# Starting the next tile's search earlier in a fused audio tower: similarities behind the search of the preceding tile, ranks behind the weights

## The chip, the cores and the metric

The kernel runs on one core of a Trainium2 chip. The metric is the device time of one execution in microseconds; less is better.

## The reference

The input is x, 16 batches of 750 x 64 float32. Per batch the model computes a token front end (four tanh layers, a convolution over 15 taps with stride 2, which leaves 375 tokens), a retention layer, a product-key attention layer, a layer with one step of test-time training, and a mixture of 8 experts. Each adds to the residual h. The change touches the third, and of it this part:

```python
sim = einsum('pbnhd,pkhd->pbnhk', q, pk_keys)          # 2 x 8 heads x 64 keys
scores, idx = top_k(sim, 16)                           # for each half
score = scores[0][..., :, None] + scores[1][..., None, :]
final_scores, pk_idx = top_k(score, 16)                # the best 16 of 256 pairs
final_scores = softmax(final_scores)
k = einsum('bnhk,bnhkd->bnhd', final_scores, keys_table[ind])
v = einsum('bnhk,bnhkd->bnhd', final_scores, values_table[ind])
attn = softmax(where(causal, einsum('bihd,bjhd->bhij', q, k), neg))
out = einsum('bhij,bjhd->bhid', attn, v) @ Wo
```

The table has 4096 rows of 64 for each of 8 heads. The training step's gradient is summed over all batches, so the last layers run only after the last batch, in a tail.

## The kernel before

**Dense instead of a gather.** Keys and values of the chosen rows are not gathered. For each head the 4096 weights of each of the 375 tokens are built densely, 128 table rows at a time (`CHUNKS` = 32), and multiplied with the table, which streams in by DMA in pieces of 8 chunks. Whether a row is chosen is told by its rank: for each first half of a key, how many second halves go with it. One chunk of one head is a *slot* (`dense_slot`), and a batch has 256 + 6 = 262 of them. A slot is on TensorE L491 (the second factor, spread out), L493 (minus a large number where the row isn't chosen), L505 (the table times the weighted rows of six slots earlier, two records) and L512 (the ranks, spread out for the next slot); on ScalarE L878 and L883; and on GpSimd L440, the product with the first factor. Slots need their head's four *factors* (`factor`: ranks, firsts and two of seconds), which TensorE transposes out of `ranks`, `firsts` and `seconds` between slots, as `factor_at` says. Each engine runs its own order, written by hand, and waits on semaphores.

**Choosing.** `pick_rows(b, t)` on VectorE works on one tile of 125 tokens; a batch has three. It is a generator, and each `yield` is a place at which other work may come between. Its steps are: the search in `rest`, the copy of the similarities (two rounds of max, index and replace over 16 groups, ending with pick step 3), the best 16 pairs (L1178 to L1202), their codes (L1205 to L1217), the ranks of four pairs of heads (L1225, three times L1231, L1235), and the weights (L1240 to L1261), which need ScalarE's exponentials (`soften`). The codes lie in one `codes` buffer and the ranks are worked out in one `picks` buffer. TensorE makes the similarities of a tile into the bank `sims` (L593), and ScalarE copies them into `rest` (`keep_similarities`, L922).

**The order of an iteration.** While batch b goes through its attention, batch b + 1 is prepared. One iteration on each engine is `attention(b)` and then `ahead(b + 2)`:
- `attention(b)`: eight heads of softmax attention over the keys and values that the slots made. In each head TensorE lays `STEPS_A` and `STEPS_B` slots beside its own work. The slots are those of batch b up to head 5, and of batch b + 1 from head 6 on (`NEXT_FROM`), which begins with `begin(b + 1)`: wait for the weights of its tile 2, and make the factors of its head 0. VectorE takes `PICKS_INSIDE` steps of tile 2 of batch b + 1 in each head.
- `prepare(b + 2)`: front end and retention, a chain of small steps through TensorE, ScalarE and VectorE. Between them come `FILL_PREPARE` slots of batch b + 1. On VectorE it begins with the squares L1112; the next instruction is the copy L1114 of the convolution's sums (L551), then the statistics, for whose deviation ScalarE waits in its order (L842).
- the similarities of tile 0, then `gradient(b)`, between whose steps come `FILL_GRADIENT` slots and seven steps of choosing of tile 0; its last sum is L1334.
- `FILL_FIRST` slots, the similarities of tile 1, `FILL_SECOND` slots, the similarities of tile 2. VectorE finishes tile 0 and then does all of tile 1.

The loop runs 14 times. `ahead(1)` stands before it, so there are 15 stages "ahead"; batch 0 is prepared and chosen first, with no slots to run beside it.

## Time and profile before

| | |
|---|---|
| median of 3 runs | 7954.98 us (7948.87 to 8025.97) |
| the profiled execution | 7943.69 us, span 7941.9 us |
| TensorE (PE) busy | 6697.2 us, 84% |
| ScalarE (ACT) busy | 5005.2 us, 63% |
| GpSimd (POOL) busy | 4498.3 us, 57% |
| VectorE (DVE) busy | 4120.9 us, 52% |
| mean granted TensorE clock | 0.941 |
| an iteration of the loop, from one L1292 to the next (3522.27 to 3994.78) | 472.5 us |

A busy share is a mean over stages with different limits. An iteration has an attention stage of about 200 us and an "ahead" of about 275 us, and each is read by itself.

### The profile page before, as it was taken

How to read it: one execution, taken by the hardware profiler on the slowest of the kernel's cores; microseconds unless marked ns; L12 is line 12 of the kernel's file. 1: busy time of each engine (PE TensorE's matmuls, PEld its weight loads, DVE VectorE, ACT ScalarE, POOL GpSimd, SP SyncE). 2: the span in 40 equal slices, each digit the busy share in tenths (PEclk: the TensorE clock that was granted, in tenths of full speed). 3: DMA queues.
4: the chain of work that ended last, by engine and by line, in shares of the span. 5: the costliest groups of instructions: out<-in, count | busy, mean ns of one | idle time of the engine just before them, and what ended most of it. 6: DMA issues, size and time to landing. Idle time of an engine off the chain costs nothing.

```text
span 7941.9 us, 139719 instructions
## 1 busy us (share of the span) xinstructions
PE 6697.2 (84%) x28800; PEld 3500.4 (44%) x28800; DVE 4120.9 (52%) x13711; ACT 5005.2 (63%) x10845; POOL 4498.3 (57%) x4108
## 2 busy tenths in 40 slices
PE   2789798897979889798888979889797988979977
PEld 1445354443535444353443535444353544435533
DVE  7472645627374472646537264562737447273146
ACT  0666576665757666576665657667575766667842
POOL 0575665656565565656556565565656556566610
PEclk9999899998999999899998989999898999999977
DMA  0111111111111111111111111111111111111100
GB/s 29 46 42 34 37 40 38 40 36 36 40 36 39 37 40 36 36 40 38 38 38 38 36 38 41 36 40 36 35 40 36 40 35 40 36 38 44 48 19 13
DMA packets 93887, 294.93 MB, mean 37 GB/s; under 512 B 17879, under 2 KB 26546, under 8 KB 92780
## 3 DMA queue, kind: packets, MB, share of 16 engines
q1 hardware_dynamic: 92748, 285.25, 11.2%
q8 instruction: 322, 5.28, 0.3%
q14 instruction: 529, 4.33, 0.2%
q10 hardware_dynamic: 288, 0.07, 0.0%
HBM read 280.68 MB, written 4.61 MB: 36 GB/s over the span
## 4 chain that ended last, share of the span: by engine, by line
PE 62%; DVE 27%; issue 6%; ACT 4%; DVEq 0%; ACTq 0%; POOL 0%; DMA 0%; SPq 0%; POOLq 0%
PE accu L505 24%; PE dense L491 7%; PE dense L512 7%; DVE picks L1231 6%; PE dense L493 6%; DVE picks L1225 4%; PE sims L623 2%; PE work L629 2%; PE sims L593 2%; DVE store L1235 2%; PE work L668 1%; DVE i L1173 1%; PE work L616 1%; PE work L551 1%; DVE picks L1205 1%
## 5 line engine op out<-in xcount | busy, mean ns | idle before, releaser
L440 POOL TENSOR_TENSOR dense_w<-dense_w,store 128x375 f32<-128x375 f32 x4096 | 4495.9, 1107 | 3092.4 <-ACT dense_w L878 3070.1
L505 PE MATMUL accu<-dense_w,store 128*128 128x375 f32 x8192 | 3365.4, 494 | 186.8 <-POOL dense_w L440 104.5
L883 ACT ACTIVATE past<-dense,edge 128x375 bf16<-128x375 f32 x4096 | 2351.8, 574 | 1195.5 <-PE dense L512 1172.5
L878 ACT ACTIVATE dense_w<-dense 128x375 f32<-128x375 f32 x4096 | 1955.5, 477 | 114.8 <-PE dense L493 107.0
L505 PEld LDWEIGHTS accu<-dense_w,store 128*128 128x128 f32 x8192 | 1430.1, 194 | 554.7 <-issue 334.9
L512 PE MATMUL dense<-store,hot 128*128 128x375 bf16 x4096 | 1338.0, 327 | 163.5 <-ACT past L883 159.4
L491 PE MATMUL dense<-store,spread 96*128 96x375 bf16 x4096 | 1353.1, 330 | 53.0 <-ACT dense_w L878 45.7
L493 PE MATMUL dense<-past,far 128*128 128x375 bf16 x4096 | 1356.8, 331 | 0.0
L512 PEld LDWEIGHTS dense<-store,hot 128*128 128x128 bf16 x4096 | 400.5, 98 | 1490.1 <-issue 1241.3
L491 PEld LDWEIGHTS dense<-store,spread 96*128 96x128 bf16 x4096 | 401.6, 98 | 839.4 <-issue 541.1
L1231 DVE TENSOR_TENSOR picks<-picks 125x2048 uint16<-125x2048 uint16 (+2 forms) x576 | 726.5, 1261 | 76.5
L593 PE MATMUL sims<-simw,n2T 64*125 64x512 f32 x192 | 151.1, 928 | 521.4 <-DVE store L1261 509.2
L1225 DVE TENSOR_TENSOR picks<-codes,keys 125x4096 uint16<-125x4096 uint16 x192 | 533.1, 2776 | 21.5
L493 PEld LDWEIGHTS dense<-past,far 128*128 128x128 bf16 x4096 | 405.3, 99 | 102.8 <-issue 29.9
L922 ACT COPY front<-sims 125x1024 f32<-125x1024 f32 x48 | 48.6, 1012 | 600.6 <-PE sims L593 600.6
L1271 DVE TENSOR_TENSOR shared<-sims,mask 125x750 f32<-125x750 f32 x64 | 59.9, 936 | 608.9 <-PE sims L623 608.9
L593 PEld LDWEIGHTS sims<-simw,n2T 64*125 64x125 f32 x192 | 47.2, 272 | 579.5 <-issue 577.6
L1292 DVE TENSOR_TENSOR h<-h_now,work 125x192 f32<-125x192 f32 x16 | 5.7, 354 | 564.9 <-PE work L677 564.9
L1235 DVE TENSOR_TENSOR store<-picks 125x256 bf16<-125x256 uint16 x192 | 190.4, 992 | 25.5
L629 PE MATMUL work<-shared 125*64 125x375 f32 (+2 forms) x768 | 190.7, 383 | 12.1 <-ACT shared L975 12.1
L623 PE MATMUL sims<-kvT,two_q 64*125 64x125 f32 (+2 forms) x768 | 194.6, 386 | 3.7 <-issue 2.5
L1281 DVE RECIPROCAL zs<-zs 125x3 f32<-125x3 f32 x128 | 22.4, 175 | 323.3 <-ACT prob_odd L944 177.0
(248 smaller groups left out, 6497.6 us busy)
## 6 DMA issues: line engine op xcount, KB each, us to landing
store<-in SPq DMA_DIRECT2D x513, 512.0 KB, 3.5
x_in<-in SPq DMA_DIRECT2D x16, 187.5 KB, 2.4
store<-in SPq DMA_DIRECT2D x1, 2048.0 KB, 8.7
queries_kept<-n3T SPq DMA_DIRECT2D x16, 93.8 KB, 3.7
h_saved<-h SPq DMA_DIRECT2D x16, 93.8 KB
store<-queries_kept SPq DMA_DIRECT2D x16, 93.8 KB, 2.3
store<-h_saved SPq DMA_DIRECT2D x16, 93.8 KB
out<-store SPq DMA_DIRECT2D x16, 93.8 KB
```

Of the source, the lines that this page charges most:

```text
L440: nc.gpsimd.tensor_tensor(dense_w[:, i % RING, :], dense_w[:, i % RING, :], first_of[:, i // CHUNKS, :], ALU.mult).then_inc(s["weighed"], 1)
L491: mm(to[:, 0:S], spread[0:3 * I1S, c % (CHUNKS // GROUPS), :], second_of[0:3 * I1S, c // (CHUNKS // GROUPS), h, :], start=True, stop=False)
L493: mm(to[:, 0:S], far[:], past[:, i % 2, :], start=False, stop=True).then_inc(s["spread"], 1)
L505: last = mm(accu[:, 0, 0:S], table[:, n % PIECE_RING, i % PIECE, :], dense_w[:, i % RING, :], start=(c == 0), stop=(c == CHUNKS - 1))
L512: mm(coded, hot[:, j % CHUNKS, :], ranksT[:, j // CHUNKS, :], start=True, stop=True).then_inc(s["coded"], 1)
L593: last = mm(sims[0:P, c, :], n2T[:, tile(t)], simw[:, c * 512:(c + 1) * 512], start=True, stop=True)
L623: last = mm(dst, qT[:, h % 2, tile(i)], kvT[0:D, h, 0:(i + 1) * P], start=True, stop=True)
L629: last = mm(work[D:128, 0, j * P:S], vo[:, j, h * D:(h + 1) * D], pT[:, min(j, 1), (0, 0, 2 * P)[j]:(S, 2 * P, S)[j]], start=(h == 0 and j ...
L878: fn(dense_w[:, i % RING, :], dense[:, n % 2, 0:S], ACT.Relu).then_inc(s["taken"], 1)
L883: fn(past[:, j % 2, :], coded, ACT.Relu, bias=edge[:, 0:1]).then_inc(s["past"], 1)
L1225: v.tensor_tensor(hit, codes[:, h:h + 2].unsqueeze(3).broadcast_to([P, 2, 2, SUB, K]), keys[:].unsqueeze(1).unsqueeze(1).broadcast_to([P, ...
L1231: v.tensor_tensor(hit[:, :, :, :, 0:m], hit[:, :, :, :, 0:m], hit[:, :, :, :, m:2 * m], ALU.min).then_inc(s["pick_step"], 1)
```

## The change

- `similarities(b, t)` for t = 1 and 2 waits for pick step 3 of tile t - 1 (its search is over) instead of its weights, the end of all its steps.
- `pick_rows`: the ranks of heads 0 and 1 stay where they were, then come the weights, and then the ranks of heads 2 to 7. A pair of heads' ranks is now an xor, one minimum and one TENSOR_REDUCE (minimum over 8), where it was an xor and four minima. `PICK_STEPS` goes from 33 to 25.
- Tile 2: 17 of its 23 steps lie inside attention, 2 or 3 a head. The other six, the ranks of heads 2 to 7, follow the squares in the next `prepare` on VectorE.
- `factor_at`: the factors of head 1 stay at slots 0 to 6; those of heads 2 to 7 begin at slot 30 (`LATER_FROM`) instead of 8. For heads 2, 4 and 6 TensorE waits for the ranks of tile 2.
- The slots are laid out anew: 29 in a preparation (36 before), 30 in a gradient (37), 48 + 64 around the similarities (26 + 43), 10 in each of heads 0 to 5 (12), 19 of the next batch in attention (36).
- The similarities of tile 1 stand 4 slots behind the gradient, those of tile 2 another 62 slots on, and 46 slots follow them. `soften` of tile 0 comes 8 slots behind the first, of tile 1 14 slots behind the second.

```diff
--- before.py
+++ after.py
@@ -35,33 +35,33 @@
 SPREAD_LAG, SUM_LAG, RING = 2, 6, 6
 SLOTS = STEPS + SUM_LAG
 FACTORS = 4
-PREPARED_EVERY = 2
+PREPARED_EVERY, LATER_FROM = 2, 30
 PIECE = 8
 PIECES = STEPS // PIECE
 PIECE_RING = 4
 I1S = 32
 GROUPS = SUB // I1S
 TAG = 256
-PIECES_A, PIECES_B = 9, 14
-PICK_STEPS = 13 + 5 * (H // 2)
+PIECES_SOON = 17
+PICK_STEPS = 13 + 3 * (H // 2)
 FAR = 1024.0
-FILL_PREPARE = (4, 3, 3, 4, 5, 4, 4, 4, 5)
-FILL_GRADIENT = (3, 6, 5, 6, 6, 6, 5)
+FILL_PREPARE = (2, 2, 2, 3, 4, 4, 4, 4, 4)
+FILL_GRADIENT = (2, 4, 4, 5, 5, 5, 5)
 PICKS_GRADIENT = (1, 1, 1, 1, 1, 1, 1)
-FILL_FIRST = (8, 18)
-FILL_SECOND = (24, 19)
+FILL_FIRST = (4, 8, 36)
+FILL_SECOND = (18, 14, 32)
 FILL_VO, FILL_QUERY, FIRST_HEAD = (2, 2, 2), 2, 4
-STEPS_A = (6, 6, 6, 6, 6, 6, 8, 8)
-STEPS_B = (6, 6, 6, 6, 6, 6, 6, 6)
+STEPS_A = (5, 5, 5, 5, 5, 5, 5, 4)
+STEPS_B = (5, 5, 5, 5, 5, 5, 4, 3)
 NEXT_FROM = 6
-FILL_LAST = (3, 5)
-PICKS_INSIDE = (4, 4, 4, 4, 4, 3, 0, 0)
+FILL_LAST = (1, 2)
+PICKS_INSIDE = (3, 3, 3, 3, 3, 2, 0, 0)
 OWN = sum(FILL_VO) + FILL_QUERY + FIRST_HEAD + sum(STEPS_A[:NEXT_FROM]) + sum(STEPS_B[:NEXT_FROM])
 EARLY = sum(STEPS_A[NEXT_FROM:]) + sum(STEPS_B[NEXT_FROM:]) + sum(FILL_LAST)
 AHEAD = sum(FILL_PREPARE) + sum(FILL_GRADIENT) + sum(FILL_FIRST) + sum(FILL_SECOND)
 assert EARLY + AHEAD + OWN == SLOTS, (EARLY, AHEAD, OWN, SLOTS)
 assert EARLY + AHEAD - SUM_LAG >= (H - LATE) * CHUNKS
-assert sum(PICKS_GRADIENT) <= PIECES_A and sum(PICKS_INSIDE) == PIECES_A + PIECES_B
+assert sum(PICKS_INSIDE) == PIECES_SOON
 
 
 class Schedule:
@@ -82,6 +82,10 @@
 
     @staticmethod
     def factor_at(j):
+        if j >= LATER_FROM:
+            j -= LATER_FROM - FACTORS * PREPARED_EVERY
+        elif j >= FACTORS * PREPARED_EVERY:
+            return None
         n, odd = divmod(j, PREPARED_EVERY)
         n += FACTORS
         return divmod(n, FACTORS) if odd == 0 and n < H * FACTORS else None
@@ -469,6 +473,8 @@
                 return dense[:, n % 2]
 
             def factor(b, h, k):
+                if h >= 2 and h % 2 == 0 and k == 0:
+                    pe.wait_ge(s["pick_step"], (b * NT + (NT - 1)) * PICK_STEPS + 13 + 3 * (h // 2 + 1))
                 to = bank_free(b, ORDER.factor[h, k])
                 for t in range(NT):
                     if k == 0:
@@ -588,7 +594,7 @@
                     pe.wait_ge(s["nT_done"], b * 2 + 2)
                 else:
                     pe.wait_ge(s["sim_kept"], b * NT + t)
-                    pe.wait_ge(s["wgt_done"], b * NT + t)
+                    pe.wait_ge(s["pick_step"], (b * NT + (t - 1)) * PICK_STEPS + 3)
                 for c in range(2):
                     last = mm(sims[0:P, c, :], n2T[:, tile(t)], simw[:, c * 512:(c + 1) * 512], start=True, stop=True)
                 last.then_inc(s["sim_mm"], 1)
@@ -734,10 +740,11 @@
                     gradient(b - 2, True)
                 else:
                     fill(b - 1, sum(FILL_GRADIENT))
-                fill(b - 1, sum(FILL_FIRST))
+                fill(b - 1, FILL_FIRST[0])
                 similarities(b, 1)
-                fill(b - 1, sum(FILL_SECOND))
+                fill(b - 1, sum(FILL_FIRST[1:]) + FILL_SECOND[0])
                 similarities(b, 2)
+                fill(b - 1, sum(FILL_SECOND[1:]))
 
             def retrieve(p, chosen):
 
@@ -1020,13 +1027,14 @@
                 else:
                     fill(b - 1, sum(FILL_GRADIENT))
                 fill(b - 1, FILL_FIRST[0])
+                keep_similarities(b, 1)
+                fill(b - 1, FILL_FIRST[1])
                 soften(b, 0)
-                fill(b - 1, FILL_FIRST[1])
-                keep_similarities(b, 1)
-                fill(b - 1, FILL_SECOND[0])
+                fill(b - 1, FILL_FIRST[2] + FILL_SECOND[0])
+                keep_similarities(b, 2)
+                fill(b - 1, FILL_SECOND[1])
                 soften(b, 1)
-                fill(b - 1, FILL_SECOND[1])
-                keep_similarities(b, 2)
+                fill(b - 1, FILL_SECOND[2])
 
             def retrieve(p, chosen):
                 for l in range(2):
@@ -1107,9 +1115,11 @@
                                            ALU.subtract, ALU.mult)
                 last.then_inc(normalised, 1)
 
-            def prepare(b):
+            def prepare(b, picking=iter(())):
                 dve.wait_ge(s["tok_act"], b * 4 + 2)
                 v.scalar_tensor_tensor(tok[:, 1], tok[:, 1], core_s[:, 0:1], tok[:, 1], ALU.mult, ALU.mult).then_inc(s["tok_sq"], 1)
+                for _ in picking:
+                    pass
                 dve.wait_ge(s["conv"], b + 1)
                 v.tensor_copy(h0[:].rearrange("p t d -> p (t d)"), work[0:P, 0, 0:NT * D]).then_inc(s["h0_done"], 1)
                 dve.wait_ge(s["h0_done"], b + 1)
@@ -1220,22 +1230,22 @@
                     dve.wait_ge(s["taken"], (b - 1) * ORDER.items + ORDER.factor[H - 1, FACTORS - 1] + 1)
                 at_step(13)
                 yield
-                for h in range(0, H, 2):
-                    k = 14 + 5 * (h // 2)
+                def ranks_of(h):
+                    k = 14 + 3 * (h // 2)
                     v.tensor_tensor(hit, codes[:, h:h + 2].unsqueeze(3).broadcast_to([P, 2, 2, SUB, K]),
                                     keys[:].unsqueeze(1).unsqueeze(1).broadcast_to([P, 2, 2, SUB, K]),
                                     ALU.bitwise_xor).then_inc(s["pick_step"], 1)
                     at_step(k)
                     yield
-                    for m in (8, 4, 2):
-                        v.tensor_tensor(hit[:, :, :, :, 0:m], hit[:, :, :, :, 0:m], hit[:, :, :, :, m:2 * m],
-                                        ALU.min).then_inc(s["pick_step"], 1)
-                        k += 1
-                        at_step(k)
-                    v.tensor_tensor(ranks[:, t, h:h + 2, :].rearrange("p h (a i) -> p h a i", a=2), hit[:, :, :, :, 0], hit[:, :, :, :, 1],
+                    v.tensor_tensor(hit[:, :, :, :, 0:K // 2], hit[:, :, :, :, 0:K // 2], hit[:, :, :, :, K // 2:],
                                     ALU.min).then_inc(s["pick_step"], 1)
                     at_step(k + 1)
+                    v.tensor_reduce(ranks[:, t, h:h + 2, :].rearrange("p h (a i) -> p h a i", a=2), hit[:, :, :, :, 0:K // 2], AX_X,
+                                    ALU.min).then_inc(s["pick_step"], 1)
+                    at_step(k + 2)
                     yield
+
+                yield from ranks_of(0)
                 dve.wait_ge(s["fexp"], n)
                 v.tensor_reduce(esum[:, 0, :], wgt[:], AX_X, ALU.add).then_inc(s["fsum"], 1)
                 dve.wait_ge(s["fsum"], n)
@@ -1259,6 +1269,9 @@
                 v.tensor_copy(seconds[:, t, :, :, 1], halves_of).then_inc(s["part_step"], 1)
                 parts(4)
                 v.tensor_tensor(seconds[:, t, :, :, 2], halves_of, seconds[:, t, :, :, 1], ALU.subtract).then_inc(s["wgt_done"], 1)
+                yield
+                for h in range(2, H, 2):
+                    yield from ranks_of(h)
 
             def pick_some(picking, n):
                 for _ in range(n):
@@ -1334,8 +1347,8 @@
                 v.tensor_tensor(grads[:], grads[:], work[0:D + 1, 1, 0:2 * D], ALU.add).then_inc(s["g_done"], 1)
                 pieces()
 
-            def ahead(b, behind):
-                prepare(b)
+            def ahead(b, behind, picking=iter(())):
+                prepare(b, picking)
                 picking = pick_rows(b, 0)
                 if behind:
                     gradient(b - 2, True, picking)
@@ -1454,9 +1467,13 @@
                     pass
             ahead(1, False)
             with nc.vector.Fori(0, B - 2) as b:
-                attention(b, pick_rows(b + 1, 2))
-                ahead(b + 2, True)
-            attention(B - 2, pick_rows(B - 1, 2))
+                picking = pick_rows(b + 1, 2)
+                attention(b, picking)
+                ahead(b + 2, True, picking)
+            picking = pick_rows(B - 1, 2)
+            attention(B - 2, picking)
+            for _ in picking:
+                pass
             gradient(B - 2, False)
             attention(B - 1)
             gradient(B - 1, False)
```

## Rows read from the trace of the kernel before

**Rows 1.** The page: busy us of each engine (share of the span), instructions.

```profile
PE 6697.2 (84%) x28800; PEld 3500.4 (44%) x28800; DVE 4120.9 (52%) x13711; ACT 5005.2 (63%) x10845; POOL 4498.3 (57%) x4108
```

**Rows 2.** Waits, whole span: who waited for whom, us in total, times, longest.

```profile
PE sims L593 <- DVE store L1261: 509.2, 31, 55.9
...
DVE h L1114 <- PE work L551: 319.4, 16, 20.4
```

**Rows 3.** TensorE timeline, 3590 to 3800 us: start, duration, instruction, idle before.

```profile
3598.84 1.95 PE L593 MATMUL sims<-simw,n2T 64*125 64x512 f32 x4 [0.79 <-ACT n2T L918]
...
3716.02 3.74 PE L593 MATMUL sims<-simw,n2T 64*125 64x512 f32 x4 [15.23 <-DVE store L1261]
...
3792.64 3.74 PE L593 MATMUL sims<-simw,n2T 64*125 64x512 f32 x4 [12.38 <-DVE store L1261]
```

**Rows 4.** What ended TensorE's idle time before L593, from 420 us on.

```profile
  DVE store L1261: 397.5, 29
```

**Rows 5.** Windows of 10 us: busy time of each engine, PEclk, DMA.

```profile
3540.00:3550.00 10.00, 8.88 (x44) 4.51 (x43) 0.00 (x0) 8.64 (x17) 4.90 (x6) 1.00 0.17 52
...
3720.00:3730.00 10.00, 10.00 (x38) 5.03 (x36) 8.67 (x73) 7.22 (x15) 6.54 (x7) 0.84 0.00 1
...
3740.00:3750.00 10.00, 10.00 (x43) 4.73 (x42) 9.41 (x63) 7.93 (x18) 7.91 (x8) 1.00 0.17 54
...
3760.00:3770.00 10.00, 7.66 (x31) 3.47 (x29) 9.12 (x7) 6.11 (x13) 10.00 (x7) 1.00 0.17 55
...
3790.00:3800.00 10.00, 6.87 (x17) 4.03 (x18) 2.05 (x4) 1.44 (x2) 0.00 (x0) 0.50 0.02 7
3800.00:3810.00 10.00, 10.00 (x49) 5.82 (x48) 0.00 (x0) 6.35 (x13) 4.63 (x5) 0.91 0.15 52
```

**Rows 6.** VectorE timeline, 3655 to 3793 us.

```profile
3657.36 0.28 DVE L1334 TENSOR_TENSOR grads<-grads,work 65x128 f32<-65x128 f32 x1 [13.90 <-PE work L719]
...
3660.93 1.17 DVE L1178 TENSOR_TENSOR cand<-s 125x128 f32<-125x128 f32 x3
...
3711.58 0.29 DVE L1240 TENSOR_REDUCE esum<-wgt 125x8 f32<-125x128 f32 x1 [0.26 <-DVE store L1235]
...
3715.18 0.69 DVE L1261 TENSOR_TENSOR store<-ex,store 125x512 bf16<-125x512 f32 x1
3721.04 2.12 DVE L1152 MAX8 s<-front 125x8 f32<-125x64 f32 x16 [5.16 <-ACT front L922]
...
3736.76 1.79 DVE L1178 TENSOR_TENSOR cand<-s 125x128 f32<-125x128 f32 x8
...
3762.33 2.85 DVE L1225 TENSOR_TENSOR picks<-codes,keys 125x4096 uint16<-125x4096 uint16 x1
...
3771.03 2.86 DVE L1225 TENSOR_TENSOR picks<-codes,keys 125x4096 uint16<-125x4096 uint16 x1
...
3791.80 0.69 DVE L1261 TENSOR_TENSOR store<-ex,store 125x512 bf16<-125x512 f32 x1
```

**Rows 7.** VectorE timeline, 80 to 93 us, GpSimd idle.

```profile
86.75 2.29 DVE L1225 TENSOR_TENSOR picks<-codes,keys 125x4096 uint16<-125x4096 uint16 x1
89.07 1.22 DVE L1231 TENSOR_TENSOR picks<-picks 125x2048 uint16<-125x2048 uint16 x1
...
92.36 2.29 DVE L1225 TENSOR_TENSOR picks<-codes,keys 125x4096 uint16<-125x4096 uint16 x1
```

**Rows 8.** VectorE, groups by shape, whole span: count, busy us, mean ns.

```profile
L1209 DVE TENSOR_REDUCE over<-picks 125x128 f32<-125x2048 f32 x48 | 109.7, 2286 | 6.5 <-DVE picks L1205 4.3
```

**Rows 9.** GpSimd timeline, 3748 to 3792 us.

```profile
3748.09 4.51 POOL L440 TENSOR_TENSOR dense_w<-dense_w,store 128x375 f32<-128x375 f32 x3 [0.22 <-ACT dense_w L878]
3753.37 33.33 POOL L440 TENSOR_TENSOR dense_w<-dense_w,store 128x375 f32<-128x375 f32 x19 [0.76 <-ACT dense_w L878]
```

**Rows 10.** VectorE timeline, 3535 to 3563 us: a preparation.

```profile
3537.55 0.61 DVE L1112 SCALAR_TENSOR_TENSOR front<-front,core_s 128x375 f32<-128x375 f32 x1 [14.93 <-ACT front L898]
3558.40 0.36 DVE L1114 COPY h<-work 125x192 f32<-125x192 f32 x1 [20.23 <-PE work L551]
```

## Prediction, made before the run

> **What bounds the kernel now.** I read the page's engine line first: TensorE is busy for 84% of the span and no other engine for more than 63% [rows 1]. So the time is TensorE's work plus the 1245 us in which it stands, and the change can gain only from the latter, from slots that run slowly, or from a cold clock. Next I read the list of waits. One entry stands out for TensorE: the similarities (L593) wait 509.2 us in 31 pieces for L1261, the last step of the preceding tile's weights [rows 2]. The answer for L593 alone gives 397.5 us of these behind 420 us, in 29 pieces [rows 4]. So 111.7 us in two pieces belong to batch 0, where nothing else is there to run, and about 397.5 / 15 = 26.5 us to each of the 15 stages "ahead". In the one I follow, 15.23 and 12.38 us, 27.6 us together [rows 3].
>
> The TensorE and VectorE timelines of that stage show why. T0 is the end of the gradient's last sum, 3657.6 us. From there VectorE works without a break on tile 0 to 3715.9 (58.3 us) and, after 5.16 us in which the next similarities travel, on tile 1 from 3721.0 to 3792.5 (71.5 us) [rows 6]. TensorE has only 5 + 26 + 43 slots of dense work to lay beside this, and runs out twice. The windows show the second cost: after each stop PEclk is 0.50, then 0.84 and 0.91, against 1.00 elsewhere [rows 5], and the four matmuls of L593 take 3.74 us at 1.2 GHz, while those of tile 0, which had no long stop ahead of them, took 1.95 us [rows 3].
>
> A slot is five matmul records. In a quiet window 43 records pass in 10 us, so a slot takes 10 / 8.6 = 1.16 us. While VectorE makes ranks it is 31 records, 6.2 slots, with GpSimd busy for the whole window [rows 5]. GpSimd's timeline gives 19 products in 33.33 us, 1.75 us each, where the ranks are made, and two whole ones beside a 2.29 us TENSOR_REDUCE (three in 4.51 us, the first of which stood behind L1205) [rows 9]. So rank making slows the slots too.
>
> **The waits that move.** The similarities of tile 1 will wait for pick step 3 of tile 0, the end of the search. In the old trace tile 1's search ends 15.7 us after its start (3721.04 to 3736.76) [rows 6]; tile 0's ended 3.3 us behind T0 (the first L1178 starts at 3660.93), most of it having been done in the gradient's places. TensorE comes to the similarities of tile 1 at 5 + 4 = 9 slots, T0 + 11 us: no stop. For tile 2 see below.
>
> **Ranks.** A pair of heads takes 8.70 us beside the products (3762.33 to 3771.03) [rows 6] and 5.61 us with GpSimd idle (86.75 to 92.36) [rows 7]: its five two-input instructions lose 0.62 us each to sharing. Afterwards there is the xor, 2.29 us alone, the first minimum, 1.22 us alone [rows 7], and a TENSOR_REDUCE of 2048 elements to 256. That form isn't in the trace. The nearest is L1209, 2048 float32 elements to 128, 2286 ns over 48 instructions, most of them beside products [rows 8]. Its bounds: 1.2 us, if 16-bit input halves it as it does the minima, and 4.6 us, twice L1209, if runs of 8 out of 16 are slow; I take 2.3. A pair then takes about 5.9 us alone and 2.29 + 1.22 + 2.3 + 2 x 0.62 + gaps = 7.2 us beside products.
>
> The row on L1209 shows a reduction of the same length in 2.29 us whether GpSimd works or not. The Trainium skill, "VectorE: DVE Perf Modes", the rule table for kernel authors, calls tensor_reduce the slowest VectorE operation and advises against it on a hot path. By that rule this edit should lose. The three instructions that it replaces take 5.61 - 2.29 - 1.22 = 2.1 us alone and 2.1 + 3 x 0.62 = 4.0 us beside products [rows 6, 7], so against 2.3 us the rule holds in batch 0 and fails everywhere else. The Trainium skill, "GPSIMD Engine Reference", says that GpSimd's memory interface is shared with VectorE's two-input instructions; GpSimd's 1.75 us against two whole products in one reduction agrees.
>
> **The stage ahead, afterwards.** VectorE from T0: tile 0 takes 58.3 - 4 x 8.7 + 4 x 7.2 = 52.3 us, and tile 1 starts at once, for its similarities are long there. Tile 1's search ends at T0 + 52 + 16 = 68. TensorE reaches the similarities of tile 2 after 5 + 4 + 8 + 36 + 18 = 71 slots: at least 71 x 1.16 + 2 = 84 us, and with rank making at 1.7 us a slot about T0 + 97. No stop, with 16 to 29 us to spare. Tile 1's other work is 71.5 - 34.8 = 36.7 us. Its weights now need ScalarE's exponentials, which come 14 slots later, at about T0 + 115, so VectorE stands some 20 us there; then 4.3 us of weights (3711.58 to 3715.9) and three pairs, 21.6 us, end at T0 + 142. TensorE needs the 117 slots, T0 + 162, before the softmax asks for VectorE. The wait costs nothing; its margin is 20 us. This stage took 139 us (T0 to the end of L593 at 3796.4) and will take about 162 with 43 more slots, worth 50 us at 1.16: a gain of 27 us and the cold clock.
>
> **Tile 2's ranks in the preparation.** Three pairs, 17.7 us alone, 21.6 beside products, now lie between the squares (L1112) and the copy of the convolution (L1114). VectorE stood there 20.23 us [rows 10], 319.4 us in 16 pieces in all [rows 2]. That cover shrinks: behind the second token matmul 3 + 3 + 4 slots become 2 + 2 + 3, 3.5 us less, and five factors leave. A factor is three or six short records, at most 0.7 us by the 0.23 us of a record in the quiet window; I take 1.5 us for the five, so 15.2 us are left. GpSimd is only half busy in such a window (4.90 of 10) [rows 5], so I take 20 us for the pairs: VectorE comes 5 us late (2.5 to 6.5). ScalarE's deviation waits behind it in order, and ScalarE's next four slots behind that, so TensorE stands for the whole of it; with some cold clock 6 us. In 14 preparations that is 84 us.
>
> **Small edits.** Attention has 10 slots a head for 12 and three pick steps for four or five; TensorE's own work of a head is unchanged, and VectorE's largest three steps (a pair's two, 7.2 us, and the first weights) stay under 10 us, and a head has 10 slots, 11.6 us, besides TensorE's own matmuls. The factors move from slots 8 to 54 to slots 30 to 76, where they lengthen the thinner fills of the gradient. The new wait in `factor` finds its ranks made: slot 30 comes behind the convolution, and its pair is the first of the three. For shorter fills at places where TensorE has to wait for ScalarE or VectorE I take 1.5 us an iteration, 22 us (0 to 90).
>
> **Sum**, against the profiled execution (7943.7 us, span 7941.9; it lies 11 us below the median of the runs):
> - recurring stops gone: -397
> - cold clock behind them: L593 2 x (3.74 - 1.95) = 3.6 us, and slots at 1.2 GHz, 10 x (1 - 0.84) + 3.6 / 2 + 10 x (1 - 0.91) = 4.3 us, 15 times: -119
> - batch 0: three pairs of tile 2 behind its weights, 3 x 5.6, and two transits of 5.2 us: -27, less 1 for the reductions: -26
> - late convolution copy: +84
> - slow slots: eight whole pairs beside pure fill, 58 us at about 1.7 us a slot, for 23 + 27 = 50 us at 1.75 before; 2 us more, 15 times: +30
> - thinner cover: +22
>
> That is -406: 7538 profiled, 7549 in the runs. I say 7550.
>
> **Rivals.** (A) The preparation costs more. If ScalarE's hold-up and the restart at 1.2 GHz cost 12 us instead of 6, the gain is 84 us less: 7635. For it: the window behind a long stop showed 0.84 and 0.91 [rows 5]. Against: the slots in front of it are few, so the pairs run nearer to 5.9 us.
> (B) The reduction holds GpSimd up as well. Then a pair lets about three products through in 7.2 us, 2.4 us a slot; 58 us pass 24 slots for 34, 11.6 us an iteration, 175 us in 15: 7725. Against it stand the two products beside L1209 [rows 9].
> (C) The change doesn't do what it says: TensorE isn't released but stops at the end of the stage, for VectorE's weights of tile 1 or the first softmax. It would keep half of the stops and clock, 260 us: 7810. Against: margins of 16 and 20 us.
> (D) Slower than before. The reduction is slow on its strided 16-bit runs by e us over 2.3. In the preparation 3e is exposed, in the stage ahead 3e less the 20 us margin. The net gain of 27 us is used up at 6e - 20 = 27, e = 8, a reduction over 10 us; at 13 us it is 6 x 10.7 - 20 = 44, 17 us an iteration the wrong way: 8200. Nothing in the trace is near four times L1209.
>
> **Chances.** Forecast (7460 to 7600) 0.62; A 0.14; B 0.08; C 0.06; D 0.03; better than 7460, if the late copy costs nothing and attention gains from its lost ranks, 0.04; within 1% of before 0.03. The range reaches over A and the bounds of the late copy and the covers: 7450 to 7690. Some 1% is what a measurement of this kernel can tell from no change: faster 0.92, same 0.04, slower 0.04.
>
> **What would show it.** In the trace after: no wait of L593 for L1261 outside batch 0, and its matmuls at 1.95 us in all tiles; the new TENSOR_REDUCE near 2.3 us; VectorE waiting some 20 us for the exponentials in tile 1; no idle time left before L1114 on VectorE but 5 to 7 us before a dense matmul on TensorE in each preparation; an iteration of about 446 us for 472.5. A long TensorE wait for L1271 would prove C, GpSimd at 2.4 us beside ranks B, a preparation stop over 10 us A.

## The result, and the profile after

The changed kernel takes 7580.06 us (median of 3 runs, 7575.18 to 7580.96), against 7954.98 us before. The ratio is 0.9501, 95% interval 0.9419 to 0.9583. I had said 7550, 7450 to 7690.

The page after, engine line first; it answers to [rows 1]:

```profile
PE 6661.1 (88%) x28800; PEld 3509.3 (46%) x28800; DVE 4020.5 (53%) x13327; ACT 5004.7 (66%) x10845; POOL 4364.7 (58%) x4108
```

TensorE is busy for 88% of a span 363 us shorter, with practically the same work. Its waits from 450 to 7000 us (who waited for whom, us in total, times, longest):

```profile
PE dense L518 <- ACT past L890: 227.1, 132, 7.4
PE accu L511 <- POOL dense_w L444: 69.2, 107, 1.1
PE work L609 <- issue: 57.3, 13, 4.9
...
PE sims L460 <- DVE nrm L1114: 41.1, 15, 3.3
...
PE sims L599 <- ACT n2T L925: 11.0, 14, 0.8
```

The entry of 397.5 us [rows 4] is gone: no similarities wait for VectorE any more. The answer for their line alone, behind 420 us (durations: least, median, greatest), shows the other half of the gain:

```profile
L599 PE MATMUL sims<-simw,n2T x168: 589/589/662, 699.7 to 6672.0; 64*125 64x512 f32 x168
```

589 ns is a matmul at 2.4 GHz, where four took 3.74 us in tiles 1 and 2 before, at 1.2 GHz [rows 3]. (`sims` in the list's fourth line is the bank of that name: its L460 is a transpose, and its wait of 41.1 us was there before too.) Two entries are to be explained: L518, a matmul of a slot that waits for ScalarE's copy `past`, 227.1 us, and L609, the first matmul of attention, behind "issue", 57.3 us in 13 pieces.

VectorE's timeline of one iteration, from one addition L1305 to the next, answers to [rows 6] and [rows 10]:

```profile
3317.25 0.35 DVE L1305 TENSOR_TENSOR h<-h_now,work 125x192 f32<-125x192 f32 x1 [19.76 <-PE work L683]
3324.50 0.61 DVE L1120 SCALAR_TENSOR_TENSOR front<-front,core_s 128x375 f32<-128x375 f32 x1 [6.90 <-ACT front L905]
3325.02 2.94 DVE L1235 TENSOR_TENSOR picks<-codes,keys 125x4096 uint16<-125x4096 uint16 x1
...
3345.43 0.36 DVE L1124 COPY h<-work 125x192 f32<-125x192 f32 x1 [0.33 <-DVE store L1243]
```
```profile
3443.90 0.28 DVE L1347 TENSOR_TENSOR grads<-grads,work 65x128 f32<-65x128 f32 x1 [13.58 <-PE work L725]
...
3486.36 2.94 DVE L1235 TENSOR_TENSOR picks<-codes,keys 125x4096 uint16<-125x4096 uint16 x1
3493.67 2.95 DVE L1235 TENSOR_TENSOR picks<-codes,keys 125x4096 uint16<-125x4096 uint16 x1
...
3558.79 0.29 DVE L1250 TENSOR_REDUCE esum<-wgt 125x8 f32<-125x128 f32 x1 [17.60 <-ACT wgt L936]
3565.39 3.07 DVE L1235 TENSOR_TENSOR picks<-codes,keys 125x4096 uint16<-125x4096 uint16 x1
...
3622.39 0.94 DVE L1284 TENSOR_TENSOR shared<-sims,mask 125x750 f32<-125x750 f32 x1 [34.65 <-PE sims L629]
```
```profile
3764.21 0.35 DVE L1305 TENSOR_TENSOR h<-h_now,work 125x192 f32<-125x192 f32 x1 [19.78 <-PE work L683]
```

The period is 3764.21 - 3317.25 = 447.0 us, for 472.5 before. The copy L1124 no longer waits for the convolution; the reduction ahead of it ends last, and the 20.23 us of idle time are gone. The pair from 3486.36 to 3493.67 takes 7.3 us. The weights of tile 1 (L1250) wait 17.60 us for ScalarE's exponentials, and VectorE has been idle for 34.65 us when the first softmax comes (L1284). I had forecast some 20 us for the first. For the second I had counted on a margin of 20 us, and it is larger. What the late copy does to TensorE and ScalarE:

```profile
3346.98 1.28 ACT L849 ACT_TABLE_LOAD   x1 [11.79 <-DVE mv L1106]
3348.27 0.30 ACT L849 ACTIVATE std<-mv,eps 125x3 f32<-125x3 f32 x1
3348.48 0.46 ACT L885 ACTIVATE dense_w<-dense 128x375 f32<-128x375 f32 x1
```
```profile
3349.55 0.47 PE L518 MATMUL dense<-store,hot 128*128 128x375 bf16 x1 [7.35 <-ACT past L890]
...
3603.43 2.33 PE L609 MATMUL work<-wo_s,kvT 64*125 64x64 f32 x10 [4.11 <-issue]
```

ScalarE stands 11.79 us for the statistics and holds its slots up meanwhile, so TensorE stands 7.35 us. The second line is the pause at the head of the loop. The same two places in the kernel before:

```profile
3562.06 0.32 PE L491 MATMUL dense<-store,spread 96*128 96x375 bf16 x1 [2.02 <-ACT dense_w L878]
...
3796.87 2.33 PE L603 MATMUL work<-wo_s,kvT 64*125 64x64 f32 x10 [0.49 <-issue]
```

Windows by stage, after and then before; columns as in [rows 5]. The stages are: to the copy of the convolution, to the gradient's last sum, to the start of attention, attention:

```profile
3317.00:3345.00 28.00, 23.95 (x122) 14.64 (x122) 19.67 (x11) 14.86 (x30) 16.30 (x12) 1.00 0.11 38
3345.00:3444.00 99.00, 82.61 (x386) 46.17 (x387) 33.98 (x150) 62.02 (x133) 43.47 (x45) 0.90 0.09 28
3444.00:3606.00 162.00, 148.23 (x610) 70.71 (x609) 117.64 (x358) 119.50 (x249) 134.31 (x117) 0.99 0.16 50
3606.00:3764.00 158.00, 148.15 (x647) 78.99 (x646) 68.98 (x282) 109.97 (x259) 80.59 (x83) 0.98 0.12 37
```
```profile
3522.00:3558.00 36.00, 33.87 (x187) 20.60 (x187) 0.97 (x2) 26.23 (x56) 17.84 (x20) 1.00 0.11 38
3558.00:3657.00 99.00, 86.26 (x368) 43.75 (x367) 33.37 (x148) 62.73 (x132) 50.90 (x54) 0.95 0.12 38
3657.00:3796.00 139.00, 99.63 (x382) 45.40 (x380) 118.87 (x374) 76.86 (x159) 100.03 (x75) 0.89 0.11 35
3796.00:3995.00 199.00, 187.86 (x835) 101.22 (x835) 93.87 (x300) 140.92 (x324) 115.41 (x109) 0.97 0.13 40
```

The first two stages take 127 us for 135, with 14 slots fewer in the fills of preparation and gradient; the third 162 for 139, with 43 more, at PEclk 0.99 for 0.89; attention 158 for 199, with fewer slots. The second stage stands out: 99 us as before, with fewer slots, at PEclk 0.90 for 0.95. Over 13 iterations of the loop its mean, from the convolution's last matmul to the gradient's, is 97.6 us at 0.96 before and 103.8 us at 0.90 after.

### The profile page after: what moved, and what is told of

Same layout as the page of the kernel before. It is cut to its first block, busy times and chain, and to the rows that moved or that the text cites. A ratio compares the mean times of both kernels' runs of the same rounds, so it can differ in the third digit from the quotient of the medians.

```text
span 7579.1 us, 138785 instructions
## 1 busy us (share of the span) xinstructions
PE 6661.1 (88%) x28800; PEld 3509.3 (46%) x28800; DVE 4020.5 (53%) x13327; ACT 5004.7 (66%) x10845; POOL 4364.7 (58%) x4108
## 4 chain that ended last, share of the span: by engine, by line
PE 76%; DVE 10%; issue 6%; ACT 6%; POOL 2%; ACTq 0%; DVEq 0%; POOLq 0%; DMA 0%; SPq 0%
PE accu L511 32%; PE dense L497 10%; PE dense L518 9%; PE dense L499 8%; PE sims L629 2%; PE work L635 2%; POOL dense_w L444 2%; DVE picks L1235 2%; PE dense L483 2%; DVE store L1243 2%; PE work L674 1%; PE work L622 1%; ACT dense_w L885 1%; PE sims L599 1%; ACT past L890 1%
## 5 line engine op out<-in xcount | busy, mean ns | idle before, releaser
L444 POOL TENSOR_TENSOR dense_w<-dense_w,store 128x375 f32<-128x375 f32 x4096 | 4362.4, 1076 | 2854.2 <-ACT dense_w L885 2821.1
L518 PE MATMUL dense<-store,hot 128*128 128x375 bf16 x4096 | 1338.0, 327 | 234.6 <-ACT past L890 234.3
L518 PEld LDWEIGHTS dense<-store,hot 128*128 128x128 bf16 x4096 | 399.3, 97 | 1572.9 <-issue 1329.2
L1284 DVE TENSOR_TENSOR shared<-sims,mask 125x750 f32<-125x750 f32 x64 | 60.1, 940 | 882.4 <-PE sims L629 882.4
L1243 DVE TENSOR_REDUCE store<-picks 125x256 bf16<-125x2048 uint16 x192 | 438.9, 2286 | 25.6 <-DVE picks L1240 6.4
L1240 DVE TENSOR_TENSOR picks<-picks 125x2048 uint16<-125x2048 uint16 x192 | 315.2, 1642 | 25.5
L1284 DVE TENSOR_TENSOR prob_odd<-sims,mask 125x750 f32<-125x750 f32 x64 | 60.0, 937 | 318.3 <-PE sims L629 318.3
L629 PE MATMUL sims<-kvT,two_q 64*125 64x125 f32 (+2 forms) x768 | 194.9, 387 | 4.7 <-issue 3.4
L946 ACT ACTIVATE two_q<-work 64x375 f32<-64x375 f32 x128 | 61.0, 476 | 171.9 <-PE work L622 171.9
L599 PE MATMUL sims<-simw,n2T 64*125 64x512 f32 x192 | 99.1, 638 | 84.5 <-DVE i L1183 68.3
L1305 DVE TENSOR_TENSOR h<-h_now,work 125x192 f32<-125x192 f32 x16 | 5.7, 354 | 310.5 <-PE work L683 310.5
L1250 DVE TENSOR_REDUCE esum<-wgt 125x8 f32<-125x128 f32 x48 | 13.7, 286 | 288.9 <-ACT wgt L936 281.4
```

Of the source, the lines that this page charges most:

```text
L444: nc.gpsimd.tensor_tensor(dense_w[:, i % RING, :], dense_w[:, i % RING, :], first_of[:, i // CHUNKS, :], ALU.mult).then_inc(s["weighed"], 1)
L518: mm(coded, hot[:, j % CHUNKS, :], ranksT[:, j // CHUNKS, :], start=True, stop=True).then_inc(s["coded"], 1)
L629: last = mm(dst, qT[:, h % 2, tile(i)], kvT[0:D, h, 0:(i + 1) * P], start=True, stop=True)
L1240: v.tensor_tensor(hit[:, :, :, :, 0:K // 2], hit[:, :, :, :, 0:K // 2], hit[:, :, :, :, K // 2:], ALU.min).then_inc(s["pick_step"], 1)
L1243: v.tensor_reduce(ranks[:, t, h:h + 2, :].rearrange("p h (a i) -> p h a i", a=2), hit[:, :, :, :, 0:K // 2], AX_X, ALU.min).then_inc(s["pi ...
```

## The experiments

Each run's time is a median of 4, and each ratio is against the kernel before on the same chip. The kernels of a group ran on one chip, where the kernel before took 7952 us (group 1), 7957 (group 2), 8011 (group 3) and 7952 (the last), so times are compared within a group first.

### Group 1: what the added parts cost

**Tile 2's ranks inside attention (e1_inside).**

```diff
-PICKS_INSIDE = (3, 3, 3, 3, 3, 2, 0, 0)
+PICKS_INSIDE = (3, 3, 3, 3, 3, 2, 2, 4)
```

> The changed kernel with the six rank steps of tile 2 taken back out of the preparation into attention's heads 6 and 7 (2 and 4 steps). Theory (the late copy of the convolution costs TensorE some 5 us of standing plus a cold clock in each of 14 preparations): the stop before the dense matmuls there falls from 7.35 to 2.0 us, the copy L1124 waits for the convolution again, and the time falls by 60 to 90 us, to about 7505. Rival (the ranks cost the same wherever they are, by holding GpSimd up or by delaying the softmax of head 7): no change within 15 us, 7565 to 7590, with the stop gone but new ones in heads 6 and 7.

7520.65 us, ratio 0.9469 (0.9433 to 0.9505), 60 us below the changed kernel's first measurement. The four runs spread from 7481 to 7549 and the intervals of the two ratios overlap, but each of the four lies below all runs of the changed kernel. The wait of L518 went from 227.1 to 154.8 us, its longest from 7.4 to 2.6:

```profile
PE dense L518 <- ACT past L890: 154.8, 131, 2.6
```

The same stage as the second of the windows above, now 97 us at PEclk 0.95 (0.93 in the mean of 13 iterations, and 97.2 us long):

```profile
3298.00:3395.00 97.00, 82.93 (x398) 45.99 (x398) 33.79 (x148) 61.79 (x133) 43.37 (x45) 0.95 0.11 34
```

So the late copy is real. It costs 60 us by the medians. By the periods of the two profiled executions, 446.3 and 440.2 us in the mean of 14, it is 85 us, but the execution profiled here was the fastest of the four. The sum had put down 84. No wait for VectorE appeared in heads 6 and 7.

**The four minima in the changed kernel (e2_minima).** Shortened: `...` stands for the leading axes, and the semaphores' steps, which follow, are left out.

```diff
-                    v.tensor_tensor(hit[..., 0:K // 2], hit[..., 0:K // 2], hit[..., K // 2:], ALU.min)
-                    v.tensor_reduce(ranks..., hit[..., 0:K // 2], AX_X, ALU.min)
+                    for m in (8, 4, 2):
+                        v.tensor_tensor(hit[..., 0:m], hit[..., 0:m], hit[..., m:2 * m], ALU.min)
+                    v.tensor_tensor(ranks..., hit[..., 0], hit[..., 1], ALU.min)
```

> The changed kernel with the four minima of before in place of one minimum and the TENSOR_REDUCE. Theory (reduction 2.29 us against 4.0 us beside products, 2.1 alone; VectorE has 20 us of margin in the stage ahead but none in the preparation): the copy comes 3 x 0 to 1.5 us later, the rank steps pass five products in 8.7 us for the reduction's four to five in 7.3, and the time rises by 20 to 80 us, to about 7625. Rival (the reduction is no help, as VectorE is off the path): within 10 us of 7580. Second rival (a reduction is the slower form): faster than 7570.

7709.58 us, ratio 0.9698 (0.9676 to 0.9721): 130 us over the changed kernel, beyond even what I expected. The reduction matters more than any theory of mine gave it.

```profile
PE dense L518 <- ACT past L890: 255.8, 132, 9.3
PE accu L511 <- POOL dense_w L444: 129.5, 145, 1.6
```

TensorE's waits for GpSimd nearly doubled, 69.2 to 129.5 us, and the stop in the preparation rose from 7.4 to 9.3 us.

**Two iterations a turn (e5_two_per_turn)**, on TensorE alone.

```diff
-            with nc.tensor.Fori(0, B - 2) as b:
-                attention(b, True)
-                ahead(b + 2, True)
+            with nc.tensor.Fori(0, (B - 2) // 2) as c:
+                for k in range(2):
+                    attention(c * 2 + k, True)
+                    ahead(c * 2 + (k + 2), True)
```

> The changed kernel with TensorE's loop of 14 turns written as 7 turns of two iterations each; the other engines keep theirs. In the trace of the changed kernel the first matmul behind the loop's jump (L609) waits for nothing but issue, 57.3 us in 13 pieces. Theory (the jump itself costs TensorE 4.4 us, which the 12 us stop of before had hidden): 7 of 13 pieces go, the time falls by 25 to 32 us, to about 7551. Rival (the pause belongs to the change of stage, to a semaphore the profile doesn't show, not to the jump): 13 pieces stay and the time is within 8 us of 7580.

7542.35 us, ratio 0.9479 (0.946 to 0.9498), 38 us below the changed kernel's first measurement, where I had expected 25 to 32. Its line of L609:

```profile
PE work L609 <- issue: 24.4, 6, 4.4
```

Six pieces for 13, as the loop has six jumps back for 13, and 32.9 us less of waiting.

**The deviation behind the slots (e6_deviation_later).**

```diff
-                deviation(b * 2 + 1, s["ln_var"], s["ln_std"])
                 between()
+                deviation(b * 2 + 1, s["ln_var"], s["ln_std"])
```

> The changed kernel with ScalarE's first deviation of each preparation placed behind its next four slots instead of ahead of them. Theory (TensorE stands 7.35 us because ScalarE, in order, waits for VectorE's late statistics and so holds up the slots): TensorE runs the four slots at once and then waits some 4 us for the normalised rows instead, 3 us less standing in all and a warmer clock, 14 times: 30 to 60 us less, about 7535. Rival (what counts is when VectorE is free, whatever ScalarE does meanwhile): TensorE stands as long as before, only 5 us further on, within 15 us of 7580.

7563.13 us, ratio 0.9507 (0.9488 to 0.9526), 17 us below the changed kernel's first measurement (ratio 0.9501), between the two theories and inside the intervals. The stop was traded, not removed:

```profile
PE dense L518 <- ACT past L890: 124.3, 118, 2.6
...
PE work L460 <- DVE nrm L1114: 71.1, 14, 5.1
```

L518 lost 103 us of waiting and L460, the transpose of the normalised rows, has 71.1 us in 14 pieces. Most of the loss follows VectorE's lateness, whoever stands in between; whether the 32 us less of waiting show in the time is open.

### Group 2: one part of the change alone

**The earlier wait alone (e3_wait_only)**, on the kernel before.

```diff
-                    pe.wait_ge(s["wgt_done"], b * NT + t)
+                    pe.wait_ge(s["pick_step"], (b * NT + (t - 1)) * PICK_STEPS + 3)
```

> The kernel before with one edit: the similarities of tiles 1 and 2 wait for pick step 3 of the preceding tile. Its layout of slots, its ranks and their order stay. Theory (the stops are TensorE waiting for all of a tile's steps, and VectorE's own length, 129.8 us from the end of the gradient to the end of tile 1, is the next limit, against some 124 us that TensorE then needs to the first softmax): no wait of L593, but a stop of 5 to 8 us at the first softmax of each attention, and some new ones where ScalarE waits for tile 1's scores; about 25 us an iteration gained, 7560 to 7640. Rival (without 43 more slots behind the similarities the stop moves whole to the first softmax, so the new layout is what brings the gain): 7850 to 7950.

7591.17 us, ratio 0.9533 (0.9483 to 0.9582). This one line, without anything else of the change, gives the time of the whole of it. The stop that I expected at the first softmax isn't there. It stands earlier, where ScalarE waits for the best scores of tile 1:

```profile
3568.21 0.47 PE L512 MATMUL dense<-store,hot 128*128 128x375 bf16 x1 [8.90 <-ACT past L883]
```
```profile
PE dense L512 <- ACT past L883: 263.0, 151, 8.9
...
PE work L603 <- issue: 30.6, 13, 2.7
```

8.7 to 8.9 us in each of 14 stages ahead, for 27.6 before.

**The reduction alone (e4_reduce_only)**, on the kernel before: the edit of the second experiment the other way round.

> The kernel before with one edit: a pair's ranks are an xor, one minimum and the TENSOR_REDUCE. Theory (a pair takes 7.2 us beside products for 8.7, so each tile ends 6 us sooner, and both stops of each stage ahead shrink by that): the wait of L593 falls from 397 to some 220 us behind batch 0, and the time by 170 to 230 us with the slots that go less slowly, to about 7750. Rival (the reduction changes VectorE's time alone and TensorE then stands elsewhere): over 7900.

7829.97 us, ratio 0.9826 (0.9766 to 0.9886): 127 us below the kernel before, where I had expected 170 to 230. The interval lies below 1, so the gain is clear in sign and not in size.

```profile
PE sims L593 <- DVE store L1259: 319.7, 29, 13.4
...
PE accu L505 <- POOL dense_w L440: 30.3, 58, 1.3
```
```profile
L440 POOL TENSOR_TENSOR dense_w<-dense_w,store 128x375 f32<-128x375 f32 x4096 | 4308.9, 1060 | 3180.1 <-ACT dense_w L878 3148.3 <-issue 4.2
```

The stops fell only from 397.5 to 319.7 us, since TensorE also reaches them sooner: its waits for GpSimd fell from 100.3 to 30.3 us. GpSimd's mean product went from 1107 ns, by the page of the kernel before, to 1060.

**The four minima in tile 2 alone (e9_minima_tile2)**, in the changed kernel.

> The changed kernel with the four minima of before in tile 2 alone, whose ranks lie in attention (one pair) and in the preparation (three). With the minima in all tiles the time was about 130 us over the changed kernel. Theory (most of it is the later copy of the convolution, 3 pairs longer by 1 us or so in the preparation, where VectorE has no margin): 40 to 70 us over the changed kernel, 7620 to 7650, with the stop in each preparation at 9 us for 7.35. Rival (most of it is the slots of the stage ahead, held up through GpSimd by eight pairs of five two-input instructions): under 30 us over the changed kernel, 7580 to 7610.

7610.49 us, ratio 0.9554 (0.9505 to 0.9602): 30 us over the changed kernel, 100 below the four minima everywhere; both of these ran on other chips. That is the upper edge of the rival's range, and outside the theory's.

```profile
PE dense L518 <- ACT past L890: 255.6, 129, 9.4
PE accu L511 <- POOL dense_w L444: 72.5, 117, 1.5
```

The stop in the preparation is as long (9.4 us) as with minima everywhere, but the waits for GpSimd are back at 72.5. So some 100 of the 130 us lie in tiles 0 and 1, beside pure dense work. The traces agree: from the gradient to the start of attention an iteration takes 160.0 us in the changed kernel, 160.8 here and 166.0 with four minima everywhere (means of 13), 6 us more in each of 15 stages.

**Ranks inside, seven iterations a turn (e8_best)**: the edits of e1_inside and of e5_two_per_turn (as 2 turns of 7) together.

> The changed kernel with tile 2's last six rank steps in attention's heads 6 and 7, and TensorE's loop as 2 turns of seven iterations. The two edits remove different waits (the stop in the preparation, 72 us and a cold clock; 12 of 13 jumps, 53 us), so theory: they add up, 60 to 100 and about 50 us below the changed kernel, 7420 to 7470. Rival (one of the two only moves the wait): 7500.

7444.82 us, ratio 0.9345 (0.9297 to 0.9393): 135 us below the changed kernel, where 60 for the ranks and some 50 for 12 of 13 jumps would be 110. The two gains add up; the rest is within the spread of the runs.

### Group 3: is the new layout needed?

**The changed kernel again (e0_again).**

> The changed kernel itself once more, so that the next two stand beside it on the same chip: 7575 to 7595.

7609.88 us, ratio 0.9511 (0.9464 to 0.9557). I had expected 7575 to 7595. This chip is slower by some 0.5% for both kernels, so the next two stand beside this number.

**The earlier wait and the reduction (e10_wait_reduce)**, on the kernel before, with its layout and its order of ranks.

> The kernel before with two edits: the earlier wait of the similarities, and one minimum and the TENSOR_REDUCE for four minima. The wait alone gave 7591, within 0.2% of the whole change, and the reduction in the changed kernel is worth 130 us. Theory (the layout with 43 more slots behind the similarities and the ranks in the preparation bring nothing of their own and cost the late copy and the exposed jump): the reduction adds its gain here too, 7450 to 7520, below the changed kernel; ScalarE's stop of 8.9 us for tile 1's scores shrinks to about 3 us. Rival (with the old layout VectorE is then the bound and the margin of the new layout is what lets the reduction count): 7560 to 7600.

7518.15 us, ratio 0.9399 (0.9353 to 0.9444): 92 us below the changed kernel on the same chip.

```profile
PE dense L512 <- ACT past L883: 238.6, 150, 7.3
...
PE work L603 <- issue: 29.7, 13, 2.7
...
PE accu L505 <- POOL dense_w L440: 9.7, 22, 1.3
```

GpSimd hardly holds TensorE up any more (9.7 us), the jump costs 29.7 us for the 58.0 of e0_again, and ScalarE's stop for the scores is 7.3 us long, where I had expected about 3.

**The same with later exponentials and seven iterations a turn (e11_wait_reduce_turns)**: `FILL_SECOND = (30, 13)` for `(24, 19)`, and the loop as 2 turns of 7.

> The same two edits, with tile 1's exponentials six slots later (FILL_SECOND 30 and 13 for 24 and 19) and TensorE's loop as 2 turns of seven iterations. Theory: the jump stood for 30.6 us in 13 pieces and the stop for tile 1's scores for what is left of it; 40 to 70 us below the run with the two edits alone, about 7430, level with the best version so far (7445) without moving a rank. Rival: the later exponentials only bring VectorE's end past the first softmax, within 30 us of the run with two edits.

7473.98 us, ratio 0.9344 (0.9298 to 0.939), 44 us below the run before, and the same ratio as e8_best without moving a rank. But here VectorE's margin is used up, as the rival had it:

```profile
PE sims L623 <- DVE shared L1270: 44.8, 9, 6.7
```

### One more: the fills

**Thick fills (e12_thick_fills)**: e8_best with the fills of before in the preparation and the gradient.

```diff
-FILL_PREPARE = (2, 2, 2, 3, 4, 4, 4, 4, 4)
-FILL_GRADIENT = (2, 4, 4, 5, 5, 5, 5)
-FILL_FIRST = (4, 8, 36)
-FILL_SECOND = (18, 14, 32)
+FILL_PREPARE = (4, 3, 3, 4, 5, 4, 4, 4, 5)
+FILL_GRADIENT = (3, 6, 5, 6, 6, 6, 5)
+FILL_FIRST = (4, 8, 29)
+FILL_SECOND = (18, 14, 25)
```

> The best version so far (tile 2's ranks in attention, seven iterations a turn; 7445, ratio 0.9345) with the preparation's and the gradient's fills as thick as before the change: 36 and 37 slots for 29 and 30, and 14 fewer around the similarities (36 to 29 and 32 to 25). Theory (thin fills between the small steps let TensorE stand more there and its clock fall; the changed kernel's PEclk in preparation and gradient is 0.92 and 0.88 against 0.96 and 0.94 before): PEclk rises towards 0.96 in both, and the time falls by 20 to 60 us, ratio 0.927 to 0.932. Rival (the clock there follows from the small steps themselves, or the factors in the fills take back what the slots cover): within 10 us, ratio 0.933 to 0.936. Second rival (VectorE's margin at the end of the stage ahead is used up): a stop of TensorE at the first softmax, slower.

7413.47 us, ratio 0.93 (0.9229 to 0.9372), the lowest time of all. Windows of the stage from the copy of the convolution to the gradient's last sum, e8_best and then e12_thick_fills:

```profile
3291.00:3388.00 97.00, 83.03 (x393) 45.14 (x392) 33.65 (x148) 61.98 (x133) 43.49 (x45) 0.93 0.11 34
```
```profile
3283.00:3385.00 102.00, 91.24 (x434) 49.10 (x433) 33.41 (x148) 69.96 (x151) 51.59 (x54) 0.95 0.11 34
```

PEclk is 0.95 for 0.93, and the waits of L518 fell from 182.6 to 124.8 us. That is the theory's direction, with less clock than it said. The intervals of the two ratios overlap, so the gain of some 30 us is likely and not shown.

## Why the prediction was right, and which terms were off

**The stops, -397: held.** None of them is left, and the margin that I had worked out for tile 2's similarities sufficed. The wait moved alone shows that this line carries the change.

**Cold clock, -119: held where it was computed, and given back elsewhere.** L599 runs warm in every tile, and the stage ahead went from PEclk 0.89 to 0.99. But the stage with preparation and gradient fell from 0.96 to 0.90 in the mean of 13 iterations. e1_inside and e8_best, which have the thin fills and not the late copy, have 0.93 and 0.92 there, so a third to a half of the fall belongs to the late copy. The thin fills' share, 0.03 to 0.04, is 2 x 0.03 x 97 = 5.8 us more at 1.2 GHz an iteration, or 7.8, worth at most half of it: 40 to 55 us in 14. I had put 22 us on the thinner covers, which is what TensorE stands more there (14.1 us in the stage of e1_inside for 12.7 before, 1.4 us an iteration), and nothing on their clock. This is the first mis-sized term.

**Batch 0, -26: held.** The first spread matmul of the dense work starts at 212.9 us for 237.5, 24.5 us sooner.

**The late copy, +84: held, within what the runs can tell.** TensorE's stop is 7.35 us for 2.02 us at that place before, 5.3 more; that is 75 us in 14. With its share of the cold clock it makes the stage 103.8 us for 97.2 in e1_inside, 6.6 us where I had taken 6. Taking the ranks away brought 60 us by the medians and 85 by the periods. The ranks ran at 20.1 us for three pairs (3325.02 to 3345.1), where I had taken 20.

**Slow slots, +30: wrong sign.** Beside the new pairs of the stage I followed GpSimd makes a product in 26.44 / 18 = 1.47 us, and not in 1.7:

```profile
3562.39 26.44 POOL L444 TENSOR_TENSOR dense_w<-dense_w,store 128x375 f32<-128x375 f32 x18
```

I had let four products through a pair of 7.2 us. Nearly five pass: 4.8 in 7.3 us, 1.52 us each, in the mean of the 73 pairs of all these stages in which GpSimd never stood, of which about 2.2 beside the reduction. Eight pairs of 7.4 us then pass some 38.5 slots in 59 us, where 1.16 us a slot would pass 51; the 50 us at 1.75 before passed 29 for 43. The loss is 12.5 slots for 14, some 1.7 us less an iteration: about -25 us where I had +30, an estimate. Four minima in tiles 0 and 1 cost some 100 us, which is the size of this term between the two forms.

**The jump, left out: +57.** TensorE's loop jump was among the costs only if one asked what the stop had hidden. Before, TensorE stood 12.4 us and then ran four slow matmuls, and the idle time before L603 was 0.49 us. In the changed kernel 4.4 us stand there 13 times. That they belong to the jump is shown by e5_two_per_turn, where 6 of the 13 are left; that the jump passed behind the stop and the slow matmuls before is my reading. The prediction asked "what is late next" of VectorE and ScalarE and not of TensorE's own sequencer.

**The rivals.** A (a dearer preparation) didn't come: the late copy with its cold clock costs 6 to 7 us an iteration and not 12, and the stop is 7.35 us and not over 10. B (the reduction holds GpSimd, 2.4 us a product) is refuted by 1.47 us. C (the stop moves to the end of the stage) didn't come. D needed a reduction over 10 us; it takes 2286 ns, the mean of 192, to the nanosecond what L1209 took [rows 8]:

```profile
L1243 DVE TENSOR_REDUCE store<-picks 125x256 bf16<-125x2048 uint16 x192 | 438.9, 2286 | 25.6 <-DVE picks L1240 6.4
```

**The reduction against the rule that I had weighed.** Alone in the kernel before it brought 127 us. The Trainium skill, "VectorE: DVE Perf Modes", its rules for kernel authors, advises against tensor_reduce on a hot path; the measurement decides otherwise where GpSimd works beside it.

**The terms against the trace.** The period fell from 469.7 to 446.3 us in the mean of 14, 328 us in all. The start gave 68 us more, of which about 20 are 17 slots that now come in the last batch; that end took 33 us more. The sum is 363 us. I had 406. The jump (57) and the clock in the thin fills (at most 40 to 55) were missing, the slots were some 55 too dear. That would make 406 - 57 - 40 + 55 = 364, or 349. So two costs that I left out are in good part made up by one that I had too dear, and the total came out better than its terms: that part is luck. Of the 33 us at the end, 20 are the slots and 6.5 the tail; the rest stays open.

**What the parts are worth.** The wait alone: 366 us. The reduction alone 127, and on top of the wait some 105 more by ratio (0.9533 to 0.9399). Wait and reduction together beat the whole change by 92 us. So the rest of it (the ranks in the preparation, the layout, the later factors) costs about that much as it stands, on that chip. Most of it is the ranks in the preparation. Without them the new layout (0.9469, 7521) and the old (0.9399, 7518) come to the same time on different chips, and by ratio the old one is ahead, with intervals that just overlap; that leaves the layout's own sign open. What speaks for the layout is VectorE's margin: with later exponentials and fewer jumps the old one has a new stop of 44.8 us at L623, and e8_best has none at L629. No run shows that this margin pays: e8_best and that run have the same ratio.

## What to carry to other kernels

When a wait stops the engine that sets the time, first ask which step of the other engine it really needs; the one line that named the end of the search in place of the end of everything gave the whole gain, and the reordering around it had to be paid for separately. When a stop goes, look for what ran unseen in its shadow, the engine's own loop jump included, and for where the work that now covers it was taken from. A reduction with one input can be worth more to a neighbour than to its own engine: count the instructions with two inputs that stand beside another engine's stream, not the microseconds.

## What the runs showed of the hardware

- GpSimd's products and VectorE's two-input instructions slow each other down. Beside five of them a pair, a product took 1.75 us in the stretch read before; beside two and a reduction 1.47 (1.52 in the mean of 73 pairs, where the 78 such pairs before have 1.69); in the quiet 0.85 to 0.98. The xor took 2.94 us beside products and 2.29 with GpSimd idle. The Trainium skill, "SBUF — State Buffer", "Who interferes with whom", says that a VectorE instruction with two inputs in SBUF contends with GpSimd's reads and that tensor_reduce never does. The trace agrees; the price in this kernel's time was 130 us of 7600.
- A TENSOR_REDUCE of 2048 16-bit elements in runs of 8 out of 16 takes 2286 ns, like one of 2048 contiguous float32 elements [rows 8]. The Trainium skill, "VectorE: DVE Perf Modes", its perf-mode tier table, gives it one speed for every type; the trace agrees.
- The jump back of a hardware loop cost TensorE 4.4 us (57.3 in 13 pieces) where dense slots stand right before it, as in the changed kernel, and 2.3 us (29.7 in 13) where the four matmuls of the similarities do, as in the old layout without the stop. With the stop and the slow matmuls, 0.4 us were left before L603 (5.2 in 13). What makes the difference wasn't tested.
- The granted clock was 0.90 in the mean of the stage from the convolution to the gradient, with one stop of 7.35 us at its head and short waits behind it. It was 0.93 and 0.92 without that stop (e1_inside, e8_best) and 0.96 with thicker fills as well (e12_thick_fills; 0.96 before).
